# Turning the weights of two streams with a permutation matmul, and a statistics matmul one part later

## What is computed

```python
def _L0_conv_ref(x, weight, bias):
    a, b, d = ...                      # from sx, sy and the angle
    q = ia * (xx * xx) + 2.0 * ib * (xx * yy) + id_ * (yy * yy)
    ker = jnp.exp(-0.5 * q)
    w = ker / jnp.sum(ker, axis=(-2, -1), keepdims=True)
    return conv(x, w, padding=4) + bias

x = x + _L0_conv_ref(_gn(x), L0_conv_weight, L0_conv_bias)
x = x + _L1_conv_ref(_gn(x), L1_conv_weight)     # 5x5, reflect padding
```

## Time and profile before

| | us |
|---|---|
| median of 3 runs | 247.71 (247.21 to 248.62) |
| profiled execution | 247.24 |
| its span, first to last instruction | 245.5 |
| TensorE busy | 228.7 |
| VectorE busy | 212.8 |
| ScalarE busy | 155.8 |
| GpSimd busy | 4.4 |

### The profile page before, as it was taken

The page is one execution under the profiler, slowest core; times in us unless marked ns, Lnnn a source line. Parts: engine busy times, 40 slices in busy tenths (PEclk is TensorE's granted clock), DMA queues, the critical chain, the costliest instruction groups (busy, mean ns, idle before and its releaser), DMA issues.

```text
span 245.5 us, 4102 instructions
## 1 busy us (share of the span) xinstructions
PE 228.7 (93%) x1409; PEld 138.9 (57%) x1409; DVE 212.8 (87%) x463; ACT 155.8 (63%) x332; POOL 4.4 (2%) x12
## 2 busy tenths in 40 slices
PE   0698499999999999999999999999999999999995
PEld 0364265555656566555666666556666665655554
DVE  4989498989999989999989999899998269978944
ACT  5887679999489845999537493456557002668310
POOL 1000000050000000000000000000000000000000
PEclk9999999999999999999999999999999999999999
DMA  6970211321005200001521100054020001530123
GB/s 185 413 310 23 64 47 43 85 56 32 0 3 145 64 4 0 0 0 48 160 98 39 61 1 3 0 139 167 4 96 3 0 0 29 153 124 38 63 96 96
DMA packets 9269, 17.77 MB, mean 72 GB/s; under 512 B 3488, under 2 KB 6176, under 8 KB 9248
## 3 DMA queue, kind: packets, MB, share of 16 engines
q1 hardware_dynamic: 8160, 16.96, 21.2%
q10 hardware_dynamic: 1088, 0.54, 0.8%
HBM read 5.57 MB, written 4.72 MB: 42 GB/s over the span
## 4 chain that ended last, share of the span: by engine, by line
PE 66%; DVE 21%; ACT 6%; issue 4%; ACTq 1%; DMA 1%; DVEq 0%
PE banks L1431 33%; PE banks L1448 32%; DVE X L769 4%; DVE lo L736 2%; ACT work L1162 2%; ACT junk L1061 2%; DVE whl L566 2%; DMA prm<-in_w 1%; DVE arg L512 1%; DVE s L498 1%; ACT hi L1117 1%; ACTq L1172 1%; DVE arg L549 1%; ACTq L1170 1%; ACT whl L1144 1%
## 5 line engine op out<-in xcount | busy, mean ns | idle before, releaser
L1431 PE MATMUL banks<-hi,whl 128*128 128x360 f16 (+4 forms) x576 | 99.3, 320 | 4.7 <-ACT hi L1117 3.5
L1431 PEld LDWEIGHTS banks<-hi,whl 128*128 128x128 f16 x576 | 55.6, 99 | 39.9 <-issue 4.1
L1431 PE MATMUL banks<-lo,whl 128*128 128x376 f16 (+4 forms) x288 | 51.6, 320 | 0.3 <-DVE lo L736 0.3
L1061 ACT ACTIVATE junk<-X 128x576 bf16<-128x576 f32 x58 | 39.6, 683 | 2.1 <-DVE X L769 0.5
L1431 PEld LDWEIGHTS banks<-lo,whl 128*128 128x128 f16 x288 | 28.0, 98 | 17.6 <-DVE lo L736 0.6
L1448 PE MATMUL banks<-lo,wh 128*128 128x384 f16 (+1 forms) x165 | 31.8, 323 | 0.0
L1448 PE MATMUL banks<-hi,wl 128*128 128x384 f16 (+1 forms) x165 | 31.8, 323 | 0.0
L1448 PE MATMUL banks<-hi,wh 128*128 128x384 f16 (+1 forms) x165 | 31.8, 323 | 0.0
L1117 ACT CAST hi<-work 128x416 f16<-128x416 f32 x32 | 16.6, 539 | 19.8 <-PE banks L1448 14.0
L1117 ACT CAST hi<-s 128x384 f16<-128x384 f32 x32 | 15.3, 509 | 19.2 <-DVE s L703 12.1
L1107 ACT ACTIVATE work<-work,gof,gsc 128x26 f32<-128x26 f32 (+1 forms) x48 | 23.4, 579 | 3.6 <-DVE gof L647 3.6
(11 more groups left out here) (134 smaller groups left out, 226.0 us busy)
## 6 DMA issues: line engine op xcount, KB each, us to landing
X<-in_x SPq DMA_DIRECT2D x8, 576.0 KB, 9.5
out<-X SPq DMA_DIRECT2D x7, 576.0 KB, 2.8
work<-X SPq DMA_DIRECT2D x8, 432.0 KB, 3.8
whl<-work SPq DMA_DIRECT2D x26, 64.0 KB, 2.0
work<-X SPq DMA_DIRECT2D x8, 144.0 KB, 3.6
stage<-in_w SPq DMA_DIRECT2D x1, 640.0 KB, 7.4
work<-X SPq DMA_DIRECT2D x32, 12.0 KB, 2.3
out<-X SPq DMA_DIRECT2D x1, 384.0 KB, 2.6
```

The costliest lines, as they stand in the source:

```text
L1061: nc.scalar.activation(waste, image(n, m), function, accum_out=sums[c][:, col:col + 1]).then_inc(sums_done[c], 1)
L1431: ins = nc.tensor.matmul(dst[:, :, o0:o1], w[1][:, i, t * P:(t + 1) * P], src[:, :, o0 + dx:o1 + dx], start=(first and part == 0 and t == ...
```

## The change

For streams 1 and 2 the turning of the partitions no longer goes through the staging buffer and transfers. ScalarE makes a permutation matrix `opposite` in f16, the identity with its four blocks of columns in reverse order. After `(1, "made")` and after `(2, "made")` TensorE multiplies it with the 512 columns of the high and of the low weights into two PSUM banks (`turn_partitions`), and ScalarE copies each result, with the column blocks reversed, straight into `whl` (`turned_kernel`). Banks 4 and 6 serve stream 1, banks 5 and 4 stream 2; the last of the four matmuls waits until bank 4 has been read. SyncE's transfers for the two streams and ScalarE's part of them (`rest_of_turn`) are gone, and with them the waits for the reuse of their staging slots. ScalarE's order is rewritten around it: the third image of `normalise1` goes ahead of the `hi` of stream 2. The table's identity columns come by a transfer of their own with a semaphore of their own. `stats(1, 1)` moves from behind `(0, "turned")` to behind `(4, "made")`.

```diff
+TURN_BANKS = {1: (4, 6), 2: (5, 4)}
@@ SyncE, turn()
-                if at == 0:
-                    sp.wait_ge(turning, 1)
-                    for k in range(RB):
-                        sp.dma_start(turned_to(i, k)[:, 0:1, :], turned_from(at, k)[:, 0:1, :]).then_inc(turned[MIRROR[i]], 16)
-                sp.wait_ge(turning, 2 * (at + 1))
-                for k in range(RB if at > 1 else RB // 2):
...
+                sp.wait_ge(turning, 2 * (at - len(TURN_BANKS) + 1))
+                for k in range(RB):
+                    sp.dma_start(whl[(RB - 1 - k) * C:(RB - k) * C, :, MIRROR[i], NT * P:],
+                                 turn_at[k * C:(k + 1) * C, at % TURNS, :, :]).then_inc(turned[MIRROR[i]], 16)
@@
             for at, i in enumerate(FIRST_ORDER):
-                turn(at, i)
+                if i not in TURN_BANKS:
+                    turn(at, i)
@@ ScalarE
-            act.dma_start(tab[:, :], tables).then_inc(tab_loaded, 16)
+            act.dma_start(tab[:, 0:TAB], tables[:, 0:TAB]).then_inc(tab_loaded, 16)
+            act.dma_start(tab[:, TAB:], tables[:, TAB:]).then_inc(identity_loaded, 16)
@@ near_factors
-                act.wait_ge(tab_loaded, 16)
+                act.wait_ge(identity_loaded, 16)
@@
+            def opposite_rows():
+                nc.scalar.copy(opposite[:, :].rearrange("p (k c) -> p k c", c=C),
+                               identity_t.rearrange("p (k c) -> p k c", c=C)[:, ::-1, :]).then_inc(opposite_made, 1)
+
+            def turned_kernel(i, half):
+                act.wait_ge(turned_mm, 2 * FIRST_ORDER.index(i) + half + 1)
+                src = banks[:, TURN_BANKS[i][half], 0:PAD1 * P].rearrange("p (b o) -> p b o", o=C)[:, ::-1, :]
+                dst = whl[:, half, MIRROR[i], NT * P:].rearrange("p (b o) -> p b o", o=C)
+                nc.scalar.copy(dst, src).then_inc(turned[i], 8 * RB)
@@
             near_factors((1, 2))
+            opposite_rows()
             kernel_exponentials()
             first_stream1()
             high_half(1, 0, 0)
             normalise1(0, range(2))
             high_kernel(1)
-            turn_kernel(1, wh)
+            normalise1(0, range(2, 3))
             high_half(1, 0, 1)
-            normalise1(0, range(2, 3))
             high_kernel_two()
-            turn_kernel(1, wl)
-            rest_of_turn(1)
+            turned_kernel(1, 0)
             normalise1(0, range(3, 4))
-            turn_kernel(2, wh)
+            turned_kernel(1, 1)
             high_kernel(0)
-            turn_kernel(2, wl)
-            rest_of_turn(2)
+            turned_kernel(2, 0)
             high_half(1, 0, 2)
+            turned_kernel(2, 1)
             turn_kernel(0, wh)
@@ TensorE, conv1
-                        pe.wait_ge(turned[i], 16 * RB)
+                        pe.wait_ge(turned[i], 8 * RB if i in TURN_BANKS else 16 * RB)
...
-                    if qd == 0 and not first and part == 2 and i == 1:
-                        pe.wait_ge(turned_low, 16 * RB)
+                    if qd == 0 and not first and part == 2 and i in TURN_BANKS:
+                        pe.wait_ge(turned[i], 16 * RB)
@@
+            def turn_partitions(i):
+                pe.wait_ge(opposite_made, 1)
+                pe.wait_ge(wl1_done, FIRST_ORDER.index(i) + 1)
+                for half, bank in enumerate(TURN_BANKS[i]):
+                    if (i, half) == (2, 1):
+                        pe.wait_ge(turned[1], 8 * RB)
+                    nc.tensor.matmul(banks[:, bank, 0:PAD1 * P], opposite[:, :], whl[:, half, i, 0:PAD1 * P],
+                                     start=True, stop=True).then_inc(turned_mm, 1)
@@
             for i, which in FIRST_PARTS:
                 first_layer1(i, which)
-                if (i, which) == (0, "turned"):
+                if i in TURN_BANKS and which == "made":
+                    turn_partitions(i)
+                if (i, which) == (4, "made"):
                     stats(1, 1)
```

More of the change, by code:

```diff
@@ L184, in build @@
                                               for k in ("msq", "var", "vare", "std", "rcp", "gsc", "gof"))
-        tab = sb("tab", [P, 2 * NE + P + NF + PAD1 + P])
+        TAB = 2 * NE + P + NF + PAD1
+        tab = sb("tab", [P, TAB + P])
         yy_t, yy2_t = (tab[:, i * NE:(i + 1) * NE] for i in range(2))
@@ L189, in build @@
         factor_t = tab[:, 2 * NE + P:2 * NE + P + NF]
-        squares_t = tab[:, 2 * NE + P + NF:2 * NE + P + NF + PAD1]
-        identity_t = tab[:, 2 * NE + P + NF + PAD1:]
+        squares_t = tab[:, 2 * NE + P + NF:TAB]
+        identity_t = tab[:, TAB:]
         factors1 = sb("factors1", [P, len(NEAR_FACTORS), P])
         off1 = sb("off1", [P, QI])
+        opposite = sb("opposite", [P, P], F16)
         osc2 = sb("osc2", [P, NF])
@@ L247, in build @@
         near_mm = sem("near_mm")
-        turned_low = sem("turned_low")
+        identity_loaded = sem("identity_loaded")
+        opposite_made = sem("opposite_made")
+        turned_mm = sem("turned_mm")
         std_done = {c: sem(f"std{c}_done") for c in (1, 2)}
@@ L333, in weight1 @@
             return block1(0) if i == 0 else block1(2) if i == 7 else slot(i)
[L335 to L339, removed]
         def made_taps(w, i):
@@ L1155, in turn_kernel @@
                 act.wait_ge(*((wh1_done, casts(i)) if part is wh else (wl1_done, at + 1)))
[L1156 to L1159, removed]
                 src = part[1][:, i, 0:PAD1 * P].rearrange("p (b o) -> p b o", o=C)[:, ::-1, :]
@@ L1496, in _ @@
             pe.wait_ge(tab_loaded, 16)
+            pe.wait_ge(identity_loaded, 16)
             for n in range(2):
```

## The result

The changed kernel takes 245.22 us in the median of six runs (243.92 to 245.85), the kernel before beside it 248.17 (247.20 to 249.17). The ratio is 0.988, with a 95% interval of 0.984 to 0.992: 2.95 us less by the medians, 3.28 by the fastest runs. I had forecast 244.3, in a range of 243.3 to 246.4.

A forecast was written before the change was run, and what follows sets the result against it. ScalarE and VectorE were taken to bound the kernel from 26.9 to 58 us. The span 245.5 less 3.15 is 242.35, 244.1 with what lies around it; 244.3 was taken as the median, range 243.3 to 246.4.

The forecast's parts named there:

- The hole and who ends it: TensorE's 3.11 us idle before 30.18 us waits for ScalarE's `hi` copy, late from issuing transfers and turn copies.
- Behind it a TensorE that never waits: Whatever moves ScalarE and VectorE earlier moves 57.91 us, after which TensorE was said never to wait.
- The pair: ScalarE and VectorE together, claimed to set the time between 26.9 and 58 us, with TensorE following.
- ScalarE's sum, 4.96 - 1.7 - 0.1: ScalarE before stream 0's `hi` copy: 4.96 us removed, 1.7 of evictions added, about 0.1 waiting; 3.15 gained.
- VectorE and ScalarE arrive together: At stream 0's `hi` copy: VectorE done at 26.3 us, ScalarE there at 26.37; faster ScalarE alone gains only 0.05.
- TensorE's added work: Four 512-column turning matmuls on TensorE, 0.43 us a pair; `(0, "made")` can then start at 27.5 us.
- The later waits: TensorE before 58 us: about 0.5 before `(5, "made")`, waits before 52.25 and 57.91 shift by 3.15, the last near 54.8.
- The statistics matmul costs nothing, and gives nothing: Moved behind `(4, "made")`: no cost, and its 0.56 us of waiting is not gained at the end.
- The identity rows: Separate load at the start lands at 6.0 to 6.4 us, delaying channel sums 0.5 to 0.9; costed at 0.
- No part of the sum is a change of clock: Granted clock reads 1.00 in every stretch, also across the 3.11 us hole, so no clock term entered.
- rival A: Smaller gain: TensorE, PSUM and ScalarE form a new waiting ring around evictions; 1.6 us gained, 245.8 median; chance 0.18.
- C: Slower: identity rows land late behind the inputs at the start, one for one beyond 6.3 us, up to 248.7; chance 0.05.

The follow-up runs named there:

- filled_after: Changed kernel with 14 constant-tile matmuls in front, five instead of two input matmuls ahead of the first statistics, and `WARMING` 12 instead of 4: 243.82 us.
- steady_stats_early: `steady_after` with the second statistics matmul put back behind `(0, "turned")`: runs of 243.81, 243.84, 245.16 and 245.34 us.
- warm_after: Changed kernel with 14 matmuls on a constant tile ahead of the first input matmuls: 243.95 us.
- steady_before: Kernel before the change with the 14 matmuls in front and five instead of two input matmuls ahead of the first statistics: 247.24 us.
- steady_after: Changed kernel with the 14 matmuls in front and five instead of two input matmuls ahead of the first statistics: 244.48 us, in two groups.

## Why the prediction was right, point by point

**The hole and who ends it.** Right. The 3.11 us were ScalarE's list, and shortening the list moved everything behind it. "Behind it a TensorE that never waits" is not quite so: the 0.4 us of idle time behind 58.0 hold the wait of 0.24 at 81.97 for ScalarE's channel sums, shown above. The pair sets the time until there, not until 57.91. That didn't harm the sum, as the whole pair moved; it is why the kernel before takes up a slow stretch of TensorE that ends at 36 us.

**ScalarE's sum, 4.96 - 1.7 - 0.1.** Right. From the head of the list to the `hi` copy it takes 26.14 - 21.92 = 4.22 us in `filled_after` instead of 7.43, which is 3.21 less. The other 0.17 of the 3.38 by which the `hi` copy moved is the head of the list, which comes at 21.92 instead of 22.09, because VectorE runs earlier with the split table. An eviction steps on by 0.48, not 0.57, and is 0.58 busy. That is 0.25 less for three, but 0.13 of it goes into waiting for VectorE behind the third, and the sum had no term for that. The Trainium skill (ScalarE: Activation LUTs, What ACT_TABLE_LOAD costs) came nearer with 0.52; its 0.61 busy for 512 columns fits the copy in SBUF (0.61) and is 0.03 above the one from PSUM (0.58).

**VectorE and ScalarE arrive together.** Right: with the clock's part taken out, VectorE's stream 0 is done at 26.10 and the `hi` copy starts at 26.14.

**TensorE's added work.** Right. 0.43 for a pair, as forecast (22.27 to 22.70 in `filled_after`), and `(0, "made")` starts at 26.74 + 4 x 0.158 = 27.4 there, forecast 27.5.

**The later waits.** Right for three of them, wrong for the last. The wait of 0.5 before `(5, "made")` is 0.70, at 43.4 (forecast 43.5), the one for `lo` stays at 0.27. The last one, forecast as a transfer near 54.8 us, is not there; TensorE stands at 56.6 behind the `hi` copy of the next quad (0.32), by the same pair, so the sum did not suffer.

**The statistics matmul costs nothing, and gives nothing.** Right, by `steady_stats_early`.

**The identity rows.** Right: the load took 4.8 us and held up `near_factors` by 0.55, and VectorE read the first statistics at 11.91, against 11.99 before. The added issue took 0.48 us of ScalarE, not 0.7. The 4.8 us of the tiny bias transfer fit a sharing of the DMA engines with the inputs, but don't show it by themselves. What I did not see is that the split lets the parameters land 0.1 earlier.

**"No part of the sum is a change of clock".** This step failed. I read the granted clock from 26.9 us on, where it is 1.00, and the tables print 1.00 ahead of that too, but the input matmuls from 8 to 11 us in the trace of before already took twice their later time. The profile before, at 247.24, was one of the executions with an early rise, near the bottom of its own range; the profile after was one with a late rise. Had I looked at the durations of the first passes, I would have had a likely reason why the three runs shown spread over 1.4 us, and a term of 0 to 2 us for both sides. I covered the spread in the range, by the 0.47 between median and profiled execution, without a cause. That the median of 245.22 falls 0.9 above the forecast and still inside the range is owed to that allowance and to the part of the range (above 245.1) that stood there for rival A, which didn't happen. That much is luck. With the late clock taken out, the sum's 244.1 stands against medians of 243.82 to 243.95.

**The rivals.** A's ring was nearly there, and not for the reason I gave. The evictions are fast; but the changed kernel has put results of TensorE on ScalarE's path, and where the clock is low while these matmuls run, ScalarE waits 1.24 us for the first and 0.21 for the third. C did not happen. That the turning itself need not be by TensorE was no rival of mine, though the sum contained it: 3.15 of the 4.96 us were the issues.

## What to carry to other kernels

Split the time that a change takes off an engine into its parts and ask for the cheapest edit that removes the largest: here ScalarE's four issues of transfers, 3.15 us, could move to an idle engine, and the new way of turning the weights on top of it brought nothing that could be measured. Compare the durations of the same matmul early and late in a trace before the first sum is made; where they differ by a factor of two, the moment of the clock's rise is in the runs' spread. A kernel gets more exposed to that clock as its holes are closed: the idle time that a change removes may have been what took up a slow stretch.

## What the runs showed of the hardware

- TensorE's clock rose from the lower to the upper level at 16 us in one execution of the changed kernel and between 13.5 and 14 in another, with spans of 243.8 and 242.6; in one of the kernel before it had risen by 11.5. It also fell again: to 0.50 from 21 to 24 us behind a wait of 2.68 us (`steady_stats_early`), at 12.4 us behind one of 1.96 (`warm_after`), and to 0.52 from 29 to 36 us behind two of 1.44 and 1.50 (`steady_before`). A wait of 3.11 us in the earlier trace rows and one of 2.55 in `steady_after` left it at 1.00, so a fall doesn't follow from each such wait.
- The granted clock in the tables reads 1.00 ahead of the rise, where four matmuls take 2.90 us instead of 1.45. A clock of 1.000 for a whole run doesn't exclude a late rise: all ten runs of the changed kernel have it, from 243.81 to 246.75 us.
- Fourteen matmuls in idle time in front cost nothing that shows: the lowest run of the kernel before is 247.14 with them and without. With the input matmuls reordered and eight more ahead of the convolution they took 1.4 us off the changed kernel's first median of 245.22, and 0.95 off its second.
- ScalarE reads 512 f32 columns from PSUM, reversed in blocks of 32, and writes f16 to SBUF in 0.58 us, a little faster than it copies 512 f16 columns in SBUF (0.61).
- An issue of one of the turning transfers holds ScalarE for 0.7 to 0.8 us, more than the copy of the data in question (0.52). The loads at the start of the changed kernel hold it for 0.44 to 0.49 each.
